# Self-attention: one PSUM bank moves from the rotation of the first scores to that of the second scores

## The chip, the cores and the metric

The kernel runs on one core of a Trainium2 chip. The metric is the device time of one execution in microseconds, given as the median of several executions. TensorE (PE in the profile) multiplies, VectorE (DVE) and ScalarE (ACT) read its results from PSUM, GpSimd (POOL) works on SBUF only, and SyncE (SP) issues most of the DMAs. PSUM has eight banks, each 128 partitions of 512 float32 values; the stage in question uses all eight.

## What is computed

One decoder block over 4 sequences of 512 tokens, 512 channels wide. The change touches the causal self-attention alone: 32 heads of 16 channels, in 8 groups of 4 heads that share keys and values.

```python
x = x + attn(layernorm(x))          # self-attention: the stage with the change
x = x + xattn(layernorm(x), ctx)    # cross-attention, 8 heads
x = x + ffn(layernorm(x))           # quantised feed-forward

# attn, per sequence b and group g:
scores = jnp.einsum('bqgjd,bkgd->bgjqk', q, k) / np.sqrt(HD)
scores = jnp.where(qpos[:, None] < qpos[None, :], -jnp.inf, scores)
w = jax.nn.softmax(scores, axis=-1)
ctx = jnp.einsum('bgjqk,bkgd->bqgjd', w, v).reshape(b, s, D) @ Wo.T
```

## The kernel before

The program is a chain of stages: projection of q, k, v (tiles named `a_`), self-attention (`b_`), output projection (`c_`), cross-attention (`d_`), feed-forward (`e_`). Each is a block of its own, and each engine has its instructions written out by hand in a fixed order. Engines meet only in semaphores.

Self-attention computes each score tile twice. The **first scores** (query rows on the partitions) exist only to find each row's maximum. The **second scores** (keys on the partitions) are computed again, with the negated maxima as two extra rows of the contraction, so that ScalarE can take the exponential and write the weights in the layout in which TensorE needs them.

There are 32 steps of first scores, one for each pair of sequence and group, and a software pipeline five steps deep. In iteration `i` of the loop (called step `i` below) the engines do:

- first scores of step `i`: ten units U0 to U9. TensorE (L609) fills one PSUM bank `b_p1` with a unit (one 512-wide tile, two of 256, or one of 128 and one of 384); VectorE (L584) adds the mask, takes the row maxima, and frees the bank (`p1_used`). U0 and U1 are F(0) and F(1) in the code, and so on.
- TURN, the transposition of the maxima of step `i - 1` (L617), which VectorE reads as two rows `b_mrow` (L576, L578). SyncE copies these into the query tile `b_qs` for the second scores of the next step.
- OUT, the transposition of the outputs of step `i - 4` (L624), which VectorE divides by the row sums (L564, L568). TURN and OUT use banks of the same rotation `b_p1`.
- second scores of step `i - 2`: eleven units S(0) to S(10) in banks `b_p2` (L638, and L641 for the diagonal masks), each read by one exponential on ScalarE (L531), which frees the bank (`exps`).
- weighting of the values with step `i - 3`: sixteen matmuls W(0) to W(3) in the one bank `b_pv` (L653), without a break; ScalarE then copies that bank to `b_osb` (L541).

VectorE takes the banks of the first rotation in this order:

```python
        ORDER = [0, 1, OUT, 2, TURN] + list(range(3, NU))
```

TensorE's order in one step, in which F waits for a free `b_p1` bank and S for a free `b_p2` bank, is:

```python
                F(0); S(0); F(1); S(1)
                turn_outputs()
                F(2); S(2)
                turn_maxima()
                F(3); S(3)
                F(4); S(4)
                W(0); W(1); W(2); W(3)
                F(5); S(5); F(6); S(6); F(7); S(7); F(8); S(8); F(9); S(9); S(10)
```

A unit may be filled when the unit that stands one rotation's length ahead of it in VectorE's order has been read. With four banks F(4) waits for OUT, since the order there is OUT, 2, TURN, 3, 4.

In the traces both rotations are called `b_p`, because numbers of buffers are left out: the line tells them apart (L609, L617 and L624 write the first rotation, L638 and L641 the second). PEld rows are weight loads; the wait of a matmul stands before its weight load.

Of the kernel before, what the change touches and what calls it, by code (L numbers as in the profile page):

```python
# [397 lines left out]
def self_attention(nc, io, scr, keep):  # L398


    STEPS = BATCH * GROUPS
    BANKS1, BANKS2 = 4, 3
    with ExitStack() as ctx:
        m = Store(nc, ctx, "b", keep["semaphores"])
        qs = m.sb("qs", [P, UNROLL, GSZ, SEQ], BF16)
# [951 lines left out]
def decoder(nc, io, out):  # L1357
# [9 lines left out]
    with ExitStack() as ctx:  # L1367
        def sb(name, shape, dt=F32):
            return ctx.enter_context(nc.sbuf_tensor(name, shape, dt))

        def sems(name, n):
            return [ctx.enter_context(nc.semaphore(f"{name}{k}")) for k in range(n)]
        keep = {
            "semaphores": ctx,


            "dve_passed": ctx.enter_context(nc.semaphore("dve_passed")), "pool_passed": ctx.enter_context(nc.semaphore("pool_passed")),
            "ident": sb("ident", [P, P]), "identb": sb("identb", [P, P], BF16), "ones64": sb("ones64", [P, XROWS]),
            "mask_qk": sb("mask_qk", [P, SEQ], BF16), "mask_kq": sb("mask_kq", [P, GSZ, P], BF16),
            "wscale": sb("wscale", [P, 3]), "winv": sb("winv", [P, 3]), "minus_half": sb("minus_half", [P, TPB]), "wo_hi": sb("wo_hi", [P, KD, DIM], F32R), "wo_lo": sb("wo_lo", [P, KD, DIM], F32R),  # L1380

            "v": sb("v", [P, BATCH * GROUPS, TPB, 2 * HDIM]),
        }
        project_qkv(nc, io, scr, keep)

        keep.update(wg=sb("wg", [P, KD, FF], BF16), wu=sb("wu", [P, KD, FF], BF16), wd=sb("wd", [P, KF, DIM], BF16))
        self_attention(nc, io, scr, keep)

        keep.update(k2=sb("k2", [P, 2, DIM]), qh=sb("qh", [P, UNROLL, DIM], F32R), ql=sb("ql", [P, UNROLL, DIM], F32R),
                    k_in=sems("k_in", 2), q_in=sems("q_in", UNROLL))  # L1390
        output_projection(nc, io, scr, keep)

        keep.update(ffn_x=sb("ffn_x", [P, XSLOTS, DIM]), ffn_x_in=sems("ffn_x_in", UNROLL))
        cross_attention(nc, io, scr, keep)
        feed_forward(nc, io, scr, keep, out)
# [32 lines left out]
```

## Time and profile before

| | us |
|---|---|
| median of 3 runs | 911.53 |
| lowest and highest | 908.85, 912.01 |
| the profiled execution | 906.05 |
| its span | 904.2 |
| PE busy | 789.2 (87%) |
| VectorE busy | 696.3 (77%) |
| ScalarE busy | 453.7 (50%) |

The span runs from the first to the last instruction, and 1.85 us of the profiled execution's time lie around it. Busy shares are means over five stages with different limits, so they say little on one stage; self-attention takes the stretch from about 101 to 403 us. Rows of the timeline give the start in us, the duration in us, the engine, the line, what is written and read, and in brackets how long the engine sat idle before it and what ended that.

### The profile page before, as it was taken

The numbers are of one execution on the slowest core, as the hardware profiler recorded it, in microseconds if no ns is written. First come the engines' busy times: TensorE is split into PE (matmuls) and PEld (weight loads), VectorE is DVE, ScalarE is ACT, GpSimd is POOL, SyncE is SP. The second block draws the span as 40 slices with busy tenths as digits, with TensorE's granted clock in tenths as the row PEclk, the third lists the DMA queues.
The fourth block names the chain that finished last, engine by engine and source line by source line (L and its number), as shares of the span: only waits on it lengthen the run. The fifth ranks groups of instructions, "written<-read, shape, count | busy, mean of one in ns | idle before, by whom it ended". The sixth has DMA issues, their size and how long they took to land. (4 is left out here: it accounts for less than half of the span.)

```text
span 904.2 us, 14319 instructions
## 1 busy us (share of the span) xinstructions
PE 789.2 (87%) x4306; PEld 404.1 (45%) x4306; DVE 696.3 (77%) x1982; ACT 453.7 (50%) x791; POOL 410.4 (45%) x412
## 2 busy tenths in 40 slices
PE   2999589999999999977884899999998379999997
PEld 1888334444444444436662444434433034444443
DVE  7554489888888889814775899898986478989984
ACT  2566147666776767652222555445544134455442
POOL 1556399999940000001223576667666323433331
PEclk9999779999999999998996899999999789999999
DMA  7987545555523223116995555655552224445443
GB/s 265 345 285 250 184 130 169 153 168 147 145 58 85 71 72 81 40 32 217 315 326 192 146 152 158 177 154 158 159 165 80 72 51 94 106 113 112 126 99 94
DMA packets 137101, 134.46 MB, mean 149 GB/s; under 512 B 87232, under 2 KB 99136, under 8 KB 133952
## 3 DMA queue, kind: packets, MB, share of 16 engines
q1 hardware_dynamic: 111488, 104.18, 39.6%
q10 hardware_dynamic: 23808, 16.78, 6.6%
q0 software_dynamic: 1728, 12.58, 4.2%
q8 instruction: 35, 0.57, 0.3%
q14 instruction: 42, 0.34, 0.1%
HBM read 89.65 MB, written 33.03 MB: 136 GB/s over the span
## 5 line engine op out<-in xcount | busy, mean ns | idle before, releaser
L584 DVE CUSTOM_DVE_ANT_0 b_junk<-b_p,mask_qk 128x128 bf16<-128x128 f32 (+3 forms) x512 | 217.7, 483 | 34.6 <-PE b_p L609 34.3
L531 ACT ACTIVATE b_probs<-b_p 128x512 f32<-128x512 f32 (+1 forms) x352 | 176.7, 560 | 49.0 <-PE b_p L641 27.2
L609 PE MATMUL b_p<-b_ks,b_qs 96*128 96x128 bf16 (+3 forms) x512 | 127.5, 314 | 16.0 <-DMA b_ks<-k_parts 10.0
L971 ACT ACTIVATE d_probs<-d_p 128x512 f32<-128x512 f32 x128 | 74.3, 594 | 106.5 <-PE d_p L1077 106.5
L638 PE MATMUL b_p<-b_qs,b_ks 98*128 98x512 bf16 (+1 forms) x352 | 123.0, 364 | 2.8 <-DMA b_qs<-b_mrow 1.8
L944 POOL TENSOR_TENSOR d_halves<-d_probs 128x1024 f32<-128x1024 f32 x32 | 76.2, 2382 | 54.0 <-ACT d_probs L971 53.9
L730 POOL TENSOR_SCALAR c_veps<-c_mv 128x1 f32<-128x1 f32 x16 | 7.1, 446 | 204.2 <-DVE c_mv L779 204.2
L995 DVE TENSOR_REDUCE d_mx<-d_p 128x1 f32<-128x512 f32 x128 | 83.7, 670 | 18.6 <-PE d_p L1060 17.5
L1341 PE MATMUL e_pg<-wg,e_xt 128*128 128x512 bf16 x256 | 67.0, 385 | 18.7 <-DMA e_xt<-e_xq 18.7
L609 PEld LDWEIGHTS b_p<-b_ks,b_qs 96*128 96x128 bf16 x512 | 45.3, 100 | 81.5 <-DVE b_mx L584 19.5
L1060 PE MATMUL d_p<-d_kk,qh 128*128 128x512 f32 x128 | 62.3, 493 | 21.6 <-DVE d_kk L1010 12.4
L653 PE MATMUL b_pv<-b_probs,v 128*32 128x512 f32 (+3 forms) x1024 | 75.5, 436 | 0.0
L1222 ACT ACTIVATE e_silu<-e_pg,e_cg 128x512 f32<-128x512 f32 x64 | 42.0, 680 | 63.9 <-PE e_pg L1341 63.9
L1106 PE MATMUL d_pn<-d_probs,d_vt 128*64 128x512 f32 x256 | 69.1, 622 | 0.0
L1341 PE MATMUL e_pu<-wu,e_xt 128*128 128x512 bf16 x256 | 66.6, 383 | 0.0
L1004 DVE RECIPROCAL d_rden<-d_pd 128x128 f32<-128x128 f32 x64 | 59.6, 938 | 7.0 <-PE d_pd L1095 6.6
L1060 PEld LDWEIGHTS d_p<-d_kk,qh 128*128 128x128 f32 x128 | 25.6, 202 | 85.2 <-issue 47.5
L1206 POOL TENSOR_SCALAR e_h<-e_h,e_fh 128x1024 f32<-128x1024 f32 x32 | 38.7, 1221 | 53.6 <-DVE e_fh L1323 53.6
L1353 PE MATMUL e_pd<-wd,e_ht 128*128 128x512 bf16 x256 | 57.7, 379 | 2.4 <-DMA e_ht<-e_hq 2.4
L1256 DVE TENSOR_TENSOR e_h<-e_pu,e_silu 128x512 f32<-128x512 f32 x64 | 43.9, 686 | 14.1 <-ACT e_silu L1222 9.6
L1076 PE MATMUL d_p<-qh,d_kk 128*128 128x512 f32 x128 | 52.4, 409 | 0.0
L1077 PE MATMUL d_p<-ql,d_kh 128*128 128x512 f32 x128 | 51.8, 405 | 0.0
(141 smaller groups left out, 1512.0 us busy)
## 6 DMA issues: line engine op xcount, KB each, us to landing
k<-in_ctx SPq DMA_DIRECT2D x64, 128.0 KB, 2.6
qh<-x_normed_high SPq DMA_DIRECT2D x64, 128.0 KB, 2.8
q_parts<-a_parts SPq DMA_DIRECT2D x16, 384.0 KB, 4.3
b_qs<-q_parts SPq DMA_DIRECT2D x32, 192.0 KB, 3.4
a_x<-in_x SPq DMA_DIRECT2D x4, 1024.0 KB, 5.6
a_wst<-in_w_gate SPq DMA_DIRECT2D x4, 1024.0 KB, 6.8
a_wst<-in_w_up SPq DMA_DIRECT2D x4, 1024.0 KB, 8.5
a_wst<-in_w_down SPq DMA_DIRECT2D x4, 1024.0 KB, 8.5
```

The source lines that it names most:

```text
L531: nc.scalar.activation(pblock(j % 2, kb)[:, j0:j0 + nj, c:c + w], p2[(NE * j + n) % BANKS2][:, 0:nj * w].rearrange("p (j c) -> p j c", j=n ...
L584: best = nc.vector.tensor_tensor_reduce(out=junk[:, 2 * ((NU * i + k) % BANKS1) + n, 0:w], in0=bank[:, c:c + w], in1=keep["mask_qk"][:, SE ...
L609: last = nc.tensor.matmul(p1_bank(i, k)[:, c:c + w], qs[0:STACK, s, j, qt * P:(qt + 1) * P], ks[0:STACK, s, 0:w], start=True, stop=True)
L638: last = nc.tensor.matmul(bank, ks[0:STACK + 2, s, kb * P:(kb + 1) * P], qs[0:STACK + 2, s, j0:j0 + nj, kb * P + c:kb * P + c + w], start= ...
L653: last = nc.tensor.matmul(pv[2 * HDIM * j:2 * HDIM * (j + 1), kb * P:], v, pblock(j3 % 2, kb)[:, j, :], start=kb == 0, stop=kb == TPB - 1, ...
L944: nc.gpsimd.tensor_tensor(halves[:], probs[:, s4, 0:2, :], probs[:, s4, 2:4, :], ALU.add).then_inc(halved, 1)
L971: nc.scalar.activation(probs[:, s3, n, :], p2[(KD * s3 + n) % BANKS][:], ACT.Exp, scale=SCALE).then_inc(exps, 1)
L995: nc.vector.reduce_max(mx[:, s1 % 2, n:n + 1], p1_bank(u, use_of(n))[:], AX.X).then_inc(p1_used, 1)
L1004: nc.vector.reciprocal(rden[:, s, at], pd[:, at]).then_inc(rden_done, 1)
L1060: nc.tensor.matmul(p1_bank(u, k)[:], qh[:, s1, n * P:(n + 1) * P], kk[:, s1, :], start=True, stop=True).then_inc(p1_full, 1)
L1106: last = nc.tensor.matmul(pn[a % 2 * H:(a % 2 + 1) * H, :], vt[:, a, nb, :], probs[:, a, nb, :], start=nb == 0, stop=nb == KD - 1, skip_gr ...
L1341: last = nc.tensor.matmul(bank[g % BANKS][:], xt[:, j % 2, k, :], keep[w][:, k, n * 512:(n + 1) * 512], start=k == 0, stop=k == KD - 1)
```

## The change

The first rotation gets three banks and the second four. The order of instructions on every engine stays as it is. What moves is which earlier reading each filling waits for. The index of VectorE's junk output, which nothing reads, also goes by `BANKS1`.

```diff
@@ -399,7 +399,7 @@
     STEPS = BATCH * GROUPS
-    BANKS1, BANKS2 = 4, 3
+    BANKS1, BANKS2 = 3, 4
```

The uses that follow from it, unchanged in their text (L595 to L597, L635 to L637):

```python
                def bank_free(k):
                    if due(USE[i, k] - BANKS1 + 1):
                        pe.wait_ge(p1_used, USE[i, k] - BANKS1 + 1)
...
                    if due(unit - BANKS2 + 1):
                        pe.wait_ge(exps, unit - BANKS2 + 1)
                    bank = p2[unit % BANKS2][:, 0:nj * w]
```

The instructions with their waits, in the program's order, differ on TensorE alone and only where a rotation is used for the first time. This is the first of the two places, in step 0, the fourth unit of first scores:

```order
 L609 MATMUL b_p<-b_ks,b_qs 128x512
 L609 MATMUL b_p<-b_ks,b_qs 128x256 x2
-L609 MATMUL b_p<-b_ks,b_qs 128x128
+L609 MATMUL b_p<-b_ks,b_qs 128x128 [waits b_p1_used]
 L609 MATMUL b_p<-b_ks,b_qs 128x384
 L609 MATMUL b_p<-b_ks,b_qs 128x512 [waits b_p1_used]
```

There the fourth unit has to wait where it had a fresh bank before. Everywhere else the same waits stand at the same instructions, with the count on the first rotation one unit higher and that on the second one unit lower. For the middle of a step this is, by the code, what each filling waits for:

| filling | before: after VectorE has read | after: after VectorE has read |
|---|---|---|
| OUT | U8 of the step before | U9 of the step before |
| F(2) | U9 of the step before | U0 |
| TURN | U0 | U1 |
| F(3) | U1 | OUT |
| F(4) | OUT | U2 |
| F(5) | U2 | TURN |

## Rows read from the trace of the kernel before

**Rows 1.** Busy time by stretch: start of self-attention, its steady part, its end.
```profile
core 0: us, PE busy (x) PEld busy (x) DVE busy (x) ACT busy (x) POOL busy (x), PEclk, DMA share, GB/s
100.00:134.00 34.00, 23.95 (x115) 9.25 (x116) 26.49 (x119) 8.12 (x17) 22.28 (x26) 0.65 0.57 167
134.00:381.00 247.00, 239.70 (x1905) 114.55 (x1903) 217.18 (x1008) 172.04 (x337) 117.80 (x131) 1.00 0.40 109
381.00:410.00 29.00, 20.65 (x164) 9.07 (x162) 6.57 (x26) 15.45 (x32) 0.00 (x0) 0.90 0.23 58
```

**Rows 2.** Timeline of VectorE through one step, 302.9 to 311.6.
```profile
302.87 0.29 DVE L584 CUSTOM_DVE_ANT_0 b_junk<-b_p,mask_qk 128x128 bf16<-128x128 f32 x1 [0.94 <-PE b_p L609]
...
306.87 0.08 DVE L584 DVE_READ_ACCUMULATOR2_ANT b_mx<- 128x1 f32 x1
...
307.48 0.08 DVE L584 DVE_READ_ACCUMULATOR2_ANT b_mx<- 128x1 f32 x1
...
307.77 0.42 DVE L568 TENSOR_TENSOR b_o<-b_p,b_rec 128x256 f32<-128x256 f32 x1
...
308.11 0.41 DVE L584 CUSTOM_DVE_ANT_0 b_junk<-b_p,mask_qk 128x256 bf16<-128x256 f32 x1
...
308.80 0.08 DVE L584 DVE_READ_ACCUMULATOR2_ANT b_mx<- 128x1 f32 x1
308.80 0.27 DVE L576 TENSOR_SCALAR b_mrow<-b_p 16x128 bf16<-16x128 f32 x1
...
309.31 0.27 DVE L584 CUSTOM_DVE_ANT_0 b_junk<-b_p,mask_qk 128x128 bf16<-128x128 f32 x1
...
310.00 0.67 DVE L584 CUSTOM_DVE_ANT_0 b_junk<-b_p,mask_qk 128x512 bf16<-128x512 f32 x1
...
310.61 0.07 DVE L584 DVE_READ_ACCUMULATOR2_ANT b_mx<- 128x1 f32 x1
...
311.61 0.29 DVE L584 CUSTOM_DVE_ANT_0 b_junk<-b_p,mask_qk 128x128 bf16<-128x128 f32 x1 [0.93 <-PE b_p L609]
```

**Rows 3.** Timeline of TensorE in the same step: F(2), TURN, F(3), F(4), W(0), F(5).
```profile
306.84 0.38 PE L609 MATMUL b_p<-b_ks,b_qs 96*128 96x256 bf16 x2
...
307.22 0.27 PE L617 MATMUL b_p<-ident,b_mx 128*16 128x128 f32 x1
...
307.62 0.11 PEld L609 LDWEIGHTS b_p<-b_ks,b_qs 96*128 96x128 bf16 x2 [0.46 <-DVE b_mx L584]
...
308.25 0.10 PEld L609 LDWEIGHTS b_p<-b_ks,b_qs 96*128 96x128 bf16 x1 [0.46 <-DVE b_o L568]
...
308.74 2.36 PE L653 MATMUL b_pv<-b_probs,v 128*32 128x512 f32 x32
...
311.03 0.39 PE L609 MATMUL b_p<-b_ks,b_qs 96*128 96x128 bf16 x2
```

**Rows 4.** The copies of b_pv on ScalarE, one a step; steps 3, 31, 32 and 34.
```profile
133.76 0.60 ACT L541 ACTIVATE b_osb<-b_pv 128x512 f32<-128x512 f32 x1 [1.83 <-PE b_pv L653]
...
381.00 0.60 ACT L541 ACTIVATE b_osb<-b_pv 128x512 f32<-128x512 f32 x1 [1.83 <-PE b_pv L653]
...
388.45 0.60 ACT L541 ACTIVATE b_osb<-b_pv 128x512 f32<-128x512 f32 x1 [1.60 <-PE b_pv L653]
...
401.17 0.60 ACT L541 ACTIVATE b_osb<-b_pv 128x512 f32<-128x512 f32 x1 [1.99 <-PE b_pv L653]
```

**Rows 5.** A step in which a load came late, at 217.8.
```profile
217.79 0.11 PEld L609 LDWEIGHTS b_p<-b_ks,b_qs 96*128 96x128 bf16 x2 [1.65 <-DMA b_ks<-k_parts]
```

**Rows 6.** Second scores waiting for an exponential: S(10) in a steady step, S(8) near the end.
```profile
304.78 0.10 PEld L638 LDWEIGHTS b_p<-b_qs,b_ks 98*128 98x128 bf16 x1 [0.19 <-ACT b_probs L531]
...
389.62 0.39 PE L638 MATMUL b_p<-b_qs,b_ks 98*128 98x512 bf16 x1 [0.25 <-ACT b_probs L531]
```

**Rows 7.** Groups by line and shape, 134 to 381 (count, busy us, mean ns, idle before).
```profile
L531 ACT ACTIVATE b_probs<-b_p 128x384 f32<-128x384 f32 x112 | 54.8, 489 | 16.5 <-PE b_p L638 12.7
...
L584 DVE CUSTOM_DVE_ANT_0 b_junk<-b_p,mask_qk 128x128 bf16<-128x128 f32 x112 | 31.7, 283 | 27.1 <-PE b_p L609 27.1
```

## Prediction before the run

> **What bounds the kernel now.** The change acts in self-attention only, so I first looked at busy time by stretch [rows 1]. In the steady part, 134 to 381 us, PE is drawn busy for 239.70 of 247.00 us and VectorE for 217.18; ScalarE with 172.04 has room. A busy PE is no proof of a bound, because the profile draws matmuls with their pipeline's length and they overlap. So the question is where each of the two stands idle, and for whom.
>
> The groups by line answer for VectorE: its 128-wide maxima have 27.1 us of idle time before them, all of it ended by a first score [rows 7]. The timeline of one step shows that this is one gap a step and nothing else: 0.94 us before the piece at 302.87, none until 310.68, and 0.93 us before the piece at 311.61 [rows 2]. That piece belongs to U5, the first unit after the weighting. VectorE thus works 7.8 us and stands 0.93 us in a period of 311.61 - 302.87 = 8.74 us.
>
> TensorE in the same step [rows 3] waits twice just ahead of the weighting: F(3) sits 0.46 us until maxima are read, F(4) sits 0.46 us until `b_o` is written, and starts at 308.25. The weighting follows at 308.74 and runs unbroken to F(5) at 311.03, and U5 reaches VectorE at 311.61. In those 2.3 us TensorE fills no bank for VectorE, which drains the four it has and then stands.
>
> So neither engine is the bound alone. The period is a ring: VectorE ends OUT (307.77 + 0.42 = 308.19), F(4) starts 0.06 later, W, F(5), U5 on VectorE, and from there VectorE's own unbroken work until it ends OUT again. Its sum is (311.61 - 308.19) + (308.19 - 302.87) = 3.42 + 5.32 = 8.74 us, the period. Any delay of F(4) lengthens it; a wait elsewhere does so only if it leaves VectorE without a full bank.
>
> **The change part by part.** Nothing is added or removed: no instruction, no DMA, no queue order. Only the waits bind to other units.
>
> *F(4), the term that decides.* It now waits for U2 instead of OUT. U2 is read as two pieces from 308.11, and the reading of its last accumulator ends at 308.80 + 0.08 = 308.88 [rows 2]. With the same 0.06 us of signalling F(4) starts at 308.94 instead of 308.25 [rows 3], 0.69 us later. S(4), the sixteen weighting matmuls and F(5) stand behind it on the same in-order engine, and U5 on VectorE waits for F(5). The ring becomes 3.42 + 5.32 + 0.69 = 9.43 us. VectorE's gap grows from 0.93 to 1.62 us; nothing hides it, as VectorE already stands idle there. The copies of `b_pv` at 133.76 and 381.00 are the first and the last of 29 (two of them shown) that belong to steps in which F(4), W and F(5) all occur, steps 3 to 31 [rows 4]. **29 x 0.69 = +20.0 us.**
>
> *The other fillings of the first rotation.* I replayed them by adding 0.06 us to the end of the new predecessor and comparing the result, plus the 0.58 us from F(5)'s start to U5's start (311.03 to 311.61) [rows 2, 3], with the moment at which VectorE comes to the unit:
> - F(2) waits for U0, whose accumulator is read until 306.95: 307.01 instead of 306.84, full by 307.59; wanted at 308.11.
> - TURN waits for U1 (307.56): 307.62 instead of 307.22, full by 308.0 (0.27 us long, and some 0.1); wanted at 308.80.
> - F(3) waits for OUT (308.19): 308.25 instead of 307.62, full by 308.83; wanted at 309.31.
> - F(4) at 308.94, full by 309.52; wanted at 310.00.
>
> All four have some 0.5 us in hand, and the units before and after them more or about as much. So these waits cost nothing: VectorE's unbroken work from U5 to U4 covers them. Without that cover the tightest would cost its excess, which is the third rival.
>
> *The second rotation.* With four banks S(10) no longer waits 0.19 us for an exponential in a steady step [rows 6], and ScalarE stands less before its 384-wide exponentials (16.5 us in all, [rows 7]). In the steady part I price this at nothing: S(10) stands where VectorE has full banks in hand, so TensorE's being 0.2 us earlier only lengthens its lead. If that cover were absent it would be worth 29 x 0.19 = 5.5 us. **0; bounds -5.5 and 0.**
>
> *The end of the stage.* From step 32 on there are no first scores. The period is 7.45 us there (388.45 - 381.00), and S does wait for exponentials, 0.25 us at 389.62 [rows 4, 6]. One more bank lets S(4), and so the weighting, start up to one exponential earlier; a 384-wide one takes 0.49 us [rows 7]. I take 0.2, 0.4 and 0.5 us for the three last weightings: **-1.1 us; bounds -1.5 and 0.**
>
> *The late loads.* From 133.76 to 381.00 are 28 periods, 247.24 us [rows 4], where 28 x 8.74 = 244.7. The 2.5 us over are a few steps in which a load for TensorE came late; the worst waited 1.65 us at the weight load [rows 5]. SyncE issues these loads when units of the step before are done, and they are wanted a step later, so a period longer by 0.69 us gives each that much more time. Most of them vanish and the worst shrinks: **-2.0 us; bounds -2.5 and 0.**
>
> *The first steps.* Steps 0 to 2 have no weighting. They wait for loads and for the slow TensorE clock (0.65 granted on the mean, [rows 1]), and VectorE there is fed unit by unit. Three banks still hold two while one is refilled. I take **+0.3 us**; bounds 0 and 3 x 0.69 = 2.1, as if each lost one unit's wait.
>
> **Sum**: 20.0 - 1.1 - 2.0 + 0.3 = +17.2 us. The profiled execution took 906.05 us, so a like one should take 923.3. That execution was 5.5 us below the median of the three runs (911.53), a scatter that I can't assign to this stage, so I add the sum to the median: **928.7 us**, 1.9% slower.
>
> **A rule weighed against the trace.** In the steady part the granted clock is 1.00, TensorE's 2.4 GHz, although TensorE has two short waits in each step; in the stretch before it, with PE drawn busy 23.95 of 34.00 us, it is 0.65, a mixture of 2.4 and 1.2 GHz [rows 1]. The Trainium skill (TensorE: Matmul & The Clock Gate, section "A second HAM failure mode: psum-queue depth-cycling") says that a kernel which cycles through PSUM banks can idle so often between groups of matmuls that its clock swings between the two levels. That speaks against this change, which makes those idle times longer. By the row the cost is nothing; by the rule it would be that of the second rival below. The new waits are 0.7 us a step in a step that keeps its 8 us of work, far nearer to the steady row than to the one before it, so I go by the row.
>
> **The rivals.**
> 1. *The freed wait of the second scores was the bound (faster).* For it: TensorE does wait for exponentials each step, and ScalarE stands 12.7 us for 384-wide second scores [rows 6, 7]. It would give -5.5 - 1.1 = -6.6 us, 904.9 us. Against it: VectorE has no idle time between U5 and U4, so a late S(10) can't be on the ring. It decides only if F(4) comes to its place after U2's end anyway, that is if TensorE ran 0.7 us later before W than the trace has it.
> 2. *The clock falls.* If TensorE fell to half speed its step would be bound by its own work: 8.74 less some 0.6 us of true waiting is about 8 us, so 16 us, 7 us more than 9.4. One step in ten (three steps) would bring 21 us: 950 us, and more if more often. For it: the first stretch. Against it: 1.00 throughout 247 us.
> 3. *VectorE runs dry at a second place.* If one of the fillings above comes 0.5 us later than my replay, VectorE loses perhaps 0.3 us more a step: +8.7, 937 us. For it: the spare time is only 0.5 us, less than one 512-wide reduction (0.67 us, [rows 2]). Against it: the order has S units of some 0.2 us between, and before this the same spaces never opened a gap.
> 4. *The new wait doesn't bind.* If something that I haven't seen held F(4) back equally before, or the end of the stage waited for other work, the change would be within 0.5% of before: about 911 us. Against it: the weight load of F(4) names `b_o` as its releaser [rows 3], and GpSimd is idle after 381 us [rows 1].
>
> **How the numbers follow.** What a measurement of this kernel can tell from no change is about 0.5%, 4.6 us. I give the forecast 0.81, rival 1 0.03, rival 2 0.05, rival 3 0.07 and rival 4 0.04. The forecast's own range: all bounds low, but for the -5.5 us, which is rival 1's, give 20.0 - 1.5 - 2.5 = 16.0, all high 20.0 + 2.1 = 22.1, so 927.5 to 933.6; with the scatter of the runs (908.85 to 912.01) 924 to 935. The range of 8 in 10 reaches from there a little to rivals 3 and 4: 921 to 937. Slower by over 0.5%: forecast and rivals 2 and 3, 0.93. Faster: 0.03. Same: 0.04.
>
> **What would show it right or wrong.** In the timeline of the changed kernel the idle time of VectorE before U5 should be 1.6 us, once a step, and the group of 128-wide maxima should show about 29 x 0.69 more idle time, some 47 us. F(4)'s weight load should name `b_mx` instead of `b_o`; F(3)'s should name `b_o`. The copies of `b_pv` should come 9.43 us apart. The wait of S(10) should be gone and the clock remain at 1.00. The prediction fails if those copies are still 8.7 us apart (rival 1 or 4), if a second gap stands in VectorE's step (rival 3), or if the granted clock of the steady part falls below 1.00 (rival 2).

## The result, and the profile after

Seven banks split three and four take 925.97 us (median of 6 runs, 923.43 to 930.51); before takes 908.62 us (median of 6, 907.27 to 912.01, the three runs shown ahead of the prediction among them). The ratio is 1.0187, 95% interval 1.0154 to 1.0221: 17.35 us slower. The profiled execution took 923.43 us with a span of 921.6.

Busy time by stretch of the changed kernel, which answers to [rows 1] (the steady part now ends near 400 us):

```profile
100.00:134.00 34.00, 23.67 (x100) 7.63 (x105) 26.65 (x119) 8.05 (x16) 22.06 (x25) 0.65 0.55 166
134.00:400.00 266.00, 248.43 (x1895) 111.69 (x1916) 216.90 (x1008) 172.69 (x337) 118.38 (x131) 1.00 0.37 101
```

VectorE does the same 217 us of work in 266 us that it did in 247. TensorE's granted clock is 1.00 as before. The two groups by line and shape that answer to [rows 7], with the weight loads of the first scores (count, busy us, mean ns, idle before):

```profile
L531 ACT ACTIVATE b_probs<-b_p 128x384 f32<-128x384 f32 x110 | 53.8, 489 | 35.0 <-PE b_p L638 35.0
...
L609 PEld LDWEIGHTS b_p<-b_ks,b_qs 96*128 96x128 bf16 x445 | 36.5, 97 | 67.6 <-DVE b_mx L584 25.3 <-DVE b_o L568 12.9 <-issue 6.1
...
L584 DVE CUSTOM_DVE_ANT_0 b_junk<-b_p,mask_qk 128x128 bf16<-128x128 f32 x111 | 31.4, 283 | 45.3 <-PE b_p L609 45.3
```

The idle time before the 128-wide maxima rose from 27.1 to 45.3 us. One step of the timeline shows where; it answers to [rows 2, 3]. The weight loads are those of F(2), TURN, F(3) and F(4), then come the weighting and F(5), then U5 on VectorE:

```profile
310.25 0.11 PEld L609 LDWEIGHTS b_p<-b_ks,b_qs 96*128 96x128 bf16 x2 [0.21 <-DVE b_mx L584]
...
310.92 0.09 PEld L617 LDWEIGHTS b_p<-ident,b_mx 128*16 128x16 f32 x1 [0.45 <-DVE b_mx L584]
...
311.49 0.11 PEld L609 LDWEIGHTS b_p<-b_ks,b_qs 96*128 96x128 bf16 x2 [0.48 <-DVE b_o L568]
...
312.04 0.08 DVE L584 DVE_READ_ACCUMULATOR2_ANT b_mx<- 128x1 f32 x1
...
312.17 0.10 PEld L609 LDWEIGHTS b_p<-b_ks,b_qs 96*128 96x128 bf16 x1 [0.51 <-DVE b_mx L584]
...
312.66 2.36 PE L653 MATMUL b_pv<-b_probs,v 128*32 128x512 f32 x32
...
314.95 0.39 PE L609 MATMUL b_p<-b_ks,b_qs 96*128 96x128 bf16 x2
...
315.53 0.29 DVE L584 CUSTOM_DVE_ANT_0 b_junk<-b_p,mask_qk 128x128 bf16<-128x128 f32 x1 [1.62 <-PE b_p L609]
...
318.02 0.38 PE L609 MATMUL b_p<-b_ks,b_qs 96*128 96x128 bf16 x2
```

F(4) sits until U2's last accumulator is read (312.04 + 0.08), starts 0.05 later, and U5 finds VectorE idle for 1.62 us instead of 0.93. The releasers moved as the table of the change says: F(3) names `b_o`, F(4) names `b_mx`.

The copies of `b_pv`, which answer to [rows 4]: two neighbours of the steady part, the last of it (step 31), and steps 32 to 34:

```profile
305.67 0.60 ACT L541 ACTIVATE b_osb<-b_pv 128x512 f32<-128x512 f32 x1 [1.83 <-PE b_pv L653]
315.09 0.60 ACT L541 ACTIVATE b_osb<-b_pv 128x512 f32<-128x512 f32 x1 [1.83 <-PE b_pv L653]
...
399.81 0.60 ACT L541 ACTIVATE b_osb<-b_pv 128x512 f32<-128x512 f32 x1 [1.83 <-PE b_pv L653]
...
406.90 0.60 ACT L541 ACTIVATE b_osb<-b_pv 128x512 f32<-128x512 f32 x1 [1.24 <-PE b_pv L653]
...
413.70 0.60 ACT L541 ACTIVATE b_osb<-b_pv 128x512 f32<-128x512 f32 x1 [1.22 <-PE b_pv L653]
...
418.75 0.60 ACT L541 ACTIVATE b_osb<-b_pv 128x512 f32<-128x512 f32 x1 [1.50 <-PE b_pv L653]
```

They give a full account. The first copy (step 3) is at 134.68, before at 133.76. In the table "late" is what the 28 periods from step 3 to 31 take over 28 times the steady period.

| | before | changed | difference |
|---|---|---|---|
| copy of step 3 | 133.76 | 134.68 | +0.92 |
| 28 steady periods | 28 x 8.73 | 28 x 9.41 | +19.0 |
| late | 2.80 | 1.65 | -1.15 |
| step 31 to 34 | 20.17 | 18.94 | -1.23 |
| copy of step 34 | 401.17 | 418.75 | +17.58 |

The spans differ by 17.4 us, so what follows self-attention takes what it took (503.0 us from the copy of step 34 to the end of the span before, 502.9 after). The large terms repeat from trace to trace. The first row and "late" don't: with four and three banks and another order (`turn_first_43`, below) the copy of step 3 is at 134.63, with three and three (`three_three`) at 135.37, and the latter's 28 periods have about 1 us over 28 x 9.41, not 1.65.

### The profile page after: what moved, and what is told of

Its sections match the earlier page's. It is cut to its first block and busy times, and to the rows that moved or that the text cites. A ratio compares the mean times of both kernels' runs of the same rounds, so it can differ in the third digit from the quotient of the medians.

```text
span 921.6 us, 14271 instructions
## 1 busy us (share of the span) xinstructions
PE 793.7 (86%) x4258; PEld 399.5 (43%) x4306; DVE 695.1 (75%) x1982; ACT 454.6 (49%) x791; POOL 411.7 (45%) x412
## 5 line engine op out<-in xcount | busy, mean ns | idle before, releaser
L1341 PE MATMUL e_pg<-wg,e_xt 128*128 128x512 bf16 x250 | 65.9, 384 | 20.0 <-DMA e_xt<-e_xq 19.7
L609 PEld LDWEIGHTS b_p<-b_ks,b_qs 96*128 96x128 bf16 x512 | 42.4, 99 | 92.4 <-DVE b_mx L584 36.7
```

The source lines that it names most:

```text
L609: last = nc.tensor.matmul(p1_bank(i, k)[:, c:c + w], qs[0:STACK, s, j, qt * P:(qt + 1) * P], ks[0:STACK, s, 0:w], start=True, stop=True)
L1341: last = nc.tensor.matmul(bank[g % BANKS][:], xt[:, j % 2, k, :], keep[w][:, k, n * 512:(n + 1) * 512], start=k == 0, stop=k == KD - 1)
```

## The experiments

**Undo half of it.** `three_three` leaves the eighth bank unused.

```diff
-    BANKS1, BANKS2 = 4, 3
+    BANKS1, BANKS2 = 3, 3
```

> Three banks for the first scores, three for the second, the eighth bank unused: half of the change. My theory (the changed kernel's time comes from F(4) waiting for U2, a ring through the weighting): the steady period is that of the changed kernel, 9.41 us between copies of b_pv, and only the gain at the stage's end is lost, so about 1.2 us above the changed kernel, 18 to 20 us above the kernel before. Rival (the fourth bank of the second scores also buys something in the steady part, up to 0.19 us a step): a period up to 9.6 us, 5 to 7 us above the changed kernel.

925.61 us, before 909.13 on the same chip, ratio 1.0192 (1.0163 to 1.0222). The steady period is 9.42 us and the last three steps take 20.18 us (420.11 - 399.93). So the fourth bank of the second scores buys 1.24 us at the end of the stage and nothing in the steady part; the whole loss is the bank taken from the first scores. The medians of this run and the changed kernel, on different chips, are too near to show the 1.2 us (925.61, 925.97); the two traces do.

**Change which unit F(4) waits for, banks untouched.** `turn_first_34` and `turn_first_43` take TURN ahead of unit 2.

```diff
-        ORDER = [0, 1, OUT, 2, TURN] + list(range(3, NU))
+        ORDER = [0, 1, OUT, TURN] + list(range(2, NU))
...
                 turn_outputs()
-                F(2); S(2)
                 turn_maxima()
+                F(2); S(2)
                 F(3); S(3)
```

> The changed kernel (three and four) with TURN moved ahead of unit 2, on TensorE and VectorE alike. The last three fillings before the weighting are then U2, U3, U4 instead of TURN, U3, U4, and F(4) waits for TURN (0.51 us) instead of U2 (0.69 us). My theory: the ring is 0.18 us shorter, a period of 9.23 us, about 5 us below the changed kernel. Rival (what costs is one bank less, not the unit that F(4) waits for): period 9.41, no difference.

> The same move of TURN in the kernel before (four and three). F(4) waits for OUT in both orders, and the four units that VectorE has left for the weighting are the same four. My theory: period 8.73 as before, no difference within 1 us. Rival (TURN's earlier place helps or harms by itself, as through the earlier copy of the maxima): a difference from the kernel before of the same size as that of the run with three and four banks from the changed kernel.

With three and four banks: 919.18 us, ratio to before 1.0110 (1.0080 to 1.0141), where the changed kernel has 1.0187, so 7 us less where 5 were expected. The period accounts for 28 x 0.18 = 5.0 us of it; the rest lies in the first copy and the late loads (step 34's copy is at 412.41 against 418.75) and is within the scatter of such runs. Its copies of `b_pv` and the weight load of F(4) in the timeline:

```profile
301.16 0.60 ACT L541 ACTIVATE b_osb<-b_pv 128x512 f32<-128x512 f32 x1 [1.83 <-PE b_pv L653]
...
307.48 0.10 PEld L609 LDWEIGHTS b_p<-b_ks,b_qs 96*128 96x128 bf16 x1 [0.33 <-DVE b_mrow L578]
...
310.39 0.60 ACT L541 ACTIVATE b_osb<-b_pv 128x512 f32<-128x512 f32 x1 [1.83 <-PE b_pv L653]
...
310.84 0.29 DVE L584 CUSTOM_DVE_ANT_0 b_junk<-b_p,mask_qk 128x128 bf16<-128x128 f32 x1 [1.43 <-PE b_p L609]
```

The period is 9.23 us, as worked out, F(4) names `b_mrow`, and the gap before U5 shrinks by the 0.19 us. With four and three banks the same move leaves the period at 8.73: 907.27 us, ratio 0.9983 (0.9968 to 0.9999). That is 1.9 us below 909.13 where less than 1 was expected; the trace shows no gain in self-attention (copy of step 34 at 402.06, before at 401.17). So with the count of banks unchanged, the period follows the unit that F(4) waits for.

**Take one bank more from the first scores.** `two_four`: two and four, one unused.

> Two banks for the first scores, four for the second, one unused: the suspected cost taken one bank further. My theory: F(4) then waits for TURN, 0.51 us of VectorE's work after U2, so the ring alone gives 9.41 + 0.51 = 9.92 us a step, 15 us above the changed kernel. That is a floor: with two banks a refill (0.06 + 0.58 us) has only one unit of 0.61 to 0.69 us to hide behind and second scores stand between, so VectorE should also run dry at other units, 30 us above the changed kernel or more. Rival (each bank taken away costs about the same, whatever waits): again about 17 us, and VectorE's idle time stays in one gap before U5.

965.09 us, ratio 1.0615 (1.0589 to 1.0642), 39 us over the changed kernel's 925.97. The steady period is 10.63 us, 0.71 above the floor of 9.92. VectorE's named idle times of one step, and its last reading of TURN:

```profile
301.94 0.29 DVE L584 CUSTOM_DVE_ANT_0 b_junk<-b_p,mask_qk 128x128 bf16<-128x128 f32 x1 [1.88 <-PE b_p L609]
...
305.65 0.29 DVE L584 CUSTOM_DVE_ANT_0 b_junk<-b_p,mask_qk 128x128 bf16<-128x128 f32 x1 [0.17 <-PE b_p L609]
...
307.24 0.26 DVE L564 RECIPROCAL b_rec<-b_p 128x16 f32<-128x16 f32 x1 [0.20 <-PE b_p L624]
...
308.87 0.28 DVE L578 SCALAR_TENSOR_TENSOR b_mrow<-b_p,b_mrow 16x128 bf16<-16x128 f32 x1
```

With three banks there was one gap; with two there are more. From U5 to the end of TURN VectorE takes 7.21 us (301.94 to 309.15), and in the kernel before 6.51 (302.87 to 309.38, the reading of TURN starting at 309.10). These 0.70 us are pauses elsewhere than before U5, two of them long enough to be named above, and F(4), which waits for TURN, is released that much later: they are the 0.71 above the floor. This is the rival "VectorE runs dry at a second place", at two banks and not at three.

**Take banks from the second scores.** `four_two` (one unused) and `five_two`, the change's opposite, which also gets ten junk slots instead of eight, so that no two maxima share one.

> Four banks for the first scores, two for the second, one unused: takes a bank from the other rotation. S(10) then waits for the exponential of S(8) instead of S(7), 0.52 us later on ScalarE, and F(0) stands behind it. TensorE's lead over VectorE there is some 0.3 us, so VectorE stands 0.2 to 0.4 us a step at U0: a period of 9.0 to 9.1, 8 to 11 us above the kernel before, plus 1 to 2 us at the stage's end. Rival (a bank of the second rotation buys nothing in the steady part at any count, as from three to four): period 8.73.

> Five banks for the first scores, two for the second: the change's opposite. F(4) waits for U1 instead of OUT, 0.63 us earlier, so the ring through the weighting alone would give 8.73 - 0.63 = 8.1 us, and VectorE's own work is 7.8. But S(10) waits for a later exponential, as in the run with four and two banks. My theory: the late second scores are then the bound, a period of 8.8 to 9.1, between 2 and 10 us above the kernel before. Rival (only the first rotation matters): 8.1 to 8.3 us, 12 us or more below the kernel before.

`four_two`: 922.11 us, before 908.63, ratio 1.0157 (1.0131 to 1.0183). `five_two`: 919.45 us, ratio 1.0126 (1.0090 to 1.0163). Steady periods 9.18 and 8.92 us; steps 31 to 34 take 23.53 us in both, 3.4 more than before. The timeline of `four_two`:

```profile
302.31 0.10 PEld L638 LDWEIGHTS b_p<-b_qs,b_ks 98*128 98x128 bf16 x1 [0.61 <-ACT b_probs L531]
...
303.33 0.29 DVE L584 CUSTOM_DVE_ANT_0 b_junk<-b_p,mask_qk 128x128 bf16<-128x128 f32 x1 [0.36 <-PE b_p L609]
...
308.77 0.29 DVE L584 CUSTOM_DVE_ANT_0 b_junk<-b_p,mask_qk 128x128 bf16<-128x128 f32 x1 [0.93 <-PE b_p L609]
```

The gap before U5 is that of before; a second one of 0.36 us opens at U0, behind a second score that waited 0.61 us for an exponential. In `five_two` the gap before U5 falls to 0.67 us, but the same 0.35 us stands at U0. I had the sign and the place right, the period by 0.1 us too low in `four_two`, and the cost at the stage's end at half its size in `four_two` and not at all in `five_two`, which is 10.8 us above before where 2 to 10 were expected. The second rotation is flat from three to four and steep from three to two.

**Break the block that F(4) stands in front of.** `split_34` and `split_43`:

```diff
                 turn_outputs()
+                W(0)
                 F(2); S(2)
                 turn_maxima()
                 F(3); S(3)
+                W(1)
                 F(4); S(4)
-                W(0); W(1); W(2); W(3)
+                W(2); W(3)
```

> The changed kernel (three and four), but TensorE's weighting is no longer one block of 2.3 us: W(0) stands behind OUT, W(1) behind S(3), W(2) and W(3) behind S(4). The same matmuls, the same waits. My theory (VectorE stands only because no bank is filled in one long block): no piece is over 0.9 us, VectorE's gap of 1.62 us mostly closes, and the step is bound by TensorE's own work, some 8.1 to 8.4 us; 29 to 38 us below the changed kernel, 11 to 20 us below the kernel before. Rival (three banks cost by themselves, through waits at each filling): a period above 9 us and slower than the kernel before.

> The kernel before (four and three) with the same split weighting. My theory: the same bound by TensorE's own work, 8.1 to 8.4 us a step; 10 to 18 us below the kernel before, and within 2 us of the run with three and four banks (which has the stage's end in its favour by 1.2 us). The cost of the change, 17 us, should be gone once the weighting is split. Rival (bank cost by itself): three and four banks still about 17 us slower than this one.

`split_34` 909.95 us, ratio to before 1.0021 (0.9986 to 1.0057); `split_43` 911.14 us, 1.0024 (0.9993 to 1.0055). Periods 8.71 and 8.68 us. The bank's cost went from 0.68 us a step to 0.03: this half of my theory holds. The gain over before didn't come: `split_34` is 16 us below the changed kernel, not 29 to 38. TensorE's timeline in `split_34` shows why; these rows are W(0), F(2), then S(2), TURN and S(3), then W(1), F(4), W(2) with W(3), F(5):

```profile
307.46 1.07 PE L653 MATMUL b_pv<-b_probs,v 128*32 128x512 f32 x8
...
308.46 0.39 PE L609 MATMUL b_p<-b_ks,b_qs 96*128 96x256 bf16 x2
...
308.69 0.33 PE L638 MATMUL b_p<-b_qs,b_ks 98*128 98x384 bf16 x1
...
308.86 0.27 PE L617 MATMUL b_p<-ident,b_mx 128*16 128x128 f32 x1
...
309.19 0.33 PE L638 MATMUL b_p<-b_qs,b_ks 98*128 98x384 bf16 x1
...
309.44 0.85 PE L653 MATMUL b_pv<-b_probs,v 128*32 128x384 f32 x8
...
310.23 0.39 PE L609 MATMUL b_p<-b_ks,b_qs 96*128 96x512 bf16 x1
...
310.71 0.86 PE L653 MATMUL b_pv<-b_probs,v 128*32 128x256 f32 x16
...
311.50 0.39 PE L609 MATMUL b_p<-b_ks,b_qs 96*128 96x128 bf16 x2
```

From start to start the pieces take 1.00 + 0.79 + 0.79 = 2.58 us, the block 2.29 [rows 3]. Each break adds about 0.15 us there. It also costs ahead of a piece: S(3) takes 0.25 us from its start to that of W(1), where S(2), of the same shape, takes 0.17 to TURN's. TensorE's matmuls follow each other without a pause in this step, so its own work is now the bound. I had left the breaks out of that work (8.1 to 8.4 expected, about 8.7 found). VectorE still stands, 0.47 us before U5 and 0.36 us at U2, but behind a busy TensorE. In `split_43` late loads add to it; more on them below.

**One break less.** `two_pieces_43` puts W(0) behind TURN and keeps W(1) to W(3) behind S(4); `two_pieces_34` has three and four banks and W(0) behind OUT.

> Four and three banks, the weighting in two pieces: W(0) behind TURN, W(1) to W(3) behind S(4). In three pieces TensorE had no idle time left in a step of 8.68 us, and the pieces took 2.58 us instead of 2.29: each break costs some 0.15 us. Two pieces should save one break: a period of 8.5, 4 to 7 us below the kernel before if the late loads don't grow. Rival (the break isn't what costs): 8.7.

> Three and four banks, the weighting in two pieces: W(0) behind OUT, W(1) to W(3) behind S(4). F(4) still waits for U2 and 1.3 us of weighting still stand behind it. The ring of the changed kernel less W(0)'s 0.9 us would be 8.5, but W(0) now stands ahead of F(2) and F(2) to F(4) come later: I expect 8.6 to 8.9, 14 to 22 us below the changed kernel and about as the kernel before, and 3 to 10 us above the run with four and three banks in two pieces: with a larger block the bank still costs. Rival (any break closes the gap as in three pieces): within 2 us of it.

`two_pieces_43`: **902.27 us**, before 908.13, ratio 0.9944 (0.9914 to 0.9974), the fastest version with the full computation. Its step:

```profile
298.21 0.60 ACT L541 ACTIVATE b_osb<-b_pv 128x512 f32<-128x512 f32 x1 [0.97 <-PE b_pv L653]
...
298.66 0.29 DVE L584 CUSTOM_DVE_ANT_0 b_junk<-b_p,mask_qk 128x128 bf16<-128x128 f32 x1 [0.64 <-PE b_p L609]
...
306.65 0.60 ACT L541 ACTIVATE b_osb<-b_pv 128x512 f32<-128x512 f32 x1 [0.97 <-PE b_pv L653]
```

The period is 8.44 us, the gap before U5 0.64. TensorE is busy throughout, as it is with three pieces; busy time by step, first `two_pieces_43`, then `split_43`:

```profile
298.21:306.65 8.44, 8.44 (x70) 4.08 (x69) 7.74 (x36) 6.05 (x13) 0.00 (x0) 1.00 0.33 78
...
301.03:309.71 8.68, 8.68 (x70) 3.94 (x69) 7.82 (x36) 6.16 (x12) 0.00 (x0) 1.00 0.30 73
```

So the second break costs 8.68 - 8.44 = 0.24 us a step, not the 0.15 that I had read from the pieces alone, and TensorE's own work with the unbroken block would be about 8.44 - 0.24 = 8.20 us (an estimate), which is inside my 8.1 to 8.4. The 28 periods gain 28 x 0.29 = 8.1 us; the late loads take 3.0 back (5.85 us over 28 regular periods, 2.80 before).

`two_pieces_34`: 917.69 us, ratio 1.0098 (1.0063 to 1.0133), period 9.01, above my 8.6 to 8.9. I placed it rightly between the changed kernel and the other, but it is only 8 us below the changed kernel (14 to 22 expected) and 15 above `two_pieces_43` (3 to 10 expected): W(0) ahead of F(2) did more harm than I allowed:

```profile
307.87 0.42 DVE L584 CUSTOM_DVE_ANT_0 b_junk<-b_p,mask_qk 128x256 bf16<-128x256 f32 x1 [0.35 <-PE b_p L609]
...
308.70 0.10 PEld L609 LDWEIGHTS b_p<-b_ks,b_qs 96*128 96x128 bf16 x1 [0.75 <-DVE b_mx L584]
```

VectorE stands 0.35 us at U2, and F(4), which waits for U2, inherits that. The two differ in where W(0) stands as well as in banks, so their 0.57 us a step is not the price of the bank alone.

**What makes loads late.** `two_loads_43` and `two_loads_split_43` drop ten of GpSimd's twelve 1 MB loads from the kernel before and from `split_43`. Both leave out most of the feed-forward's weights, so they serve as measurements only.

```diff
-                    if c + 1 < 3 * LOADS:
+                    if c + 1 < 2:
                         load(c + 1)
-                    pool.wait_ge(wst_in[c % 2], 16 * (c // 2 + 1))
+                    pool.wait_ge(wst_in[c % 2], 16)
```

> The kernel before, without ten of the twelve 1 MB loads of feed-forward weights that GpSimd issues during self-attention (the feed-forward then works with two slices of weights only; the number of instructions on the compute engines is unchanged). In both traces all late loads of the attention's own tiles lie between 106 and 243 us, where these 1 MB loads are issued, one each 12.4 us. My theory: they are what makes the others late; without them the 28 periods from step 3 have next to no excess over 28 x 8.73 (2.8 us before) and the first steps gain 1 to 2 us: 3 to 5 us below the kernel before. Rival (late by their own queue's order on SyncE): the excess stays at 2 to 3 us.

> The same omission in the run with four and three banks and the weighting in three pieces, whose 28 periods had 9.9 us of excess over 28 x 8.68. My theory: the excess goes, the steady period stays 8.68, and the time falls by 8 to 12 us. Rival (late by their own queue's order): excess stays near 10 us.

904.95 us, ratio 0.9961 (0.9943 to 0.9979), and 902.72 us, ratio 0.9939 (0.9919 to 0.9959), both to before. The excess of `split_43` was 9.9 us in its profile and is 0.0 here, with the period at 8.68. GpSimd's own work is not what changed: from 134 to 170 us it is busy for 33.95 us in the kernel before and for 34.02 without the loads.

Not all of the 9.9 us is waiting. Two steps hold 7.7 of it, 12.71 and 12.37 us long, and in both the granted clock fell. This is the busy time of the first, and the weighting W(0) in it:

```profile
152.27:164.98 12.71, 10.65 (x70) 4.14 (x69) 8.09 (x36) 6.16 (x13) 12.00 (x14) 0.87 0.50 157
...
159.18 1.94 PE L653 MATMUL b_pv<-b_probs,v 128*32 128x512 f32 x8
```

TensorE had stood 1.95 us for a load just before 157.32. Then the granted clock fell to 0.50 (1.2 GHz) between 160 and 162 us, and W(0) took 1.94 us instead of 1.06. TensorE was busy for 10.65 us in this step, where the regular one has 8.68; in the second (granted clock 0.86) for 10.47, after a stand of 1.90 us. So some 3.8 of the 9.9 us are the slower clock, which a sum of the waits misses. Without the 1 MB loads the granted clock is 1.00 from 134 us on. In `two_pieces_43` a stand of 2.13 us left the clock at 1.00, so such a stand doesn't always lower it.

In the kernel before the excess falls from 2.8 to 0.93 us. The 0.93 left sits in the same four steps in six of the nine runs with the weighting in one block (not in `two_four`, `four_two` and `five_two`). In the one of these steps that I looked at, in the kernel before, 0.22 of its 0.31 us is a pause inside VectorE's stretch that no engine or load ends:

```profile
242.35 0.69 DVE L584 CUSTOM_DVE_ANT_0 b_junk<-b_p,mask_qk 128x512 bf16<-128x512 f32 x1 [0.22 <-issue]
```

So of "late" in the table above, some 1.9 us before and, if the same 0.93 stays, 0.7 us after were loads that those 1 MB loads delay. What the pause is stays open.

## Why the prediction was right

- **F(4) and the ring.** Predicted 29 x 0.69 = 20.0 us and a period of 9.43; measured 9.41 against 8.73, so 28 x 0.68, and the 29th is in the copy of step 3: 19.7 us. The experiments back the cause and not only the size: three and three banks give the same period, moving TURN changes it by just the difference of the two units' durations with three banks and not at all with four, and cutting the weighting up removes the cost.
- **The other fillings cost nothing.** Replayed starts, with the changed times shifted by 3.25 us (U5, which opens the step, was at 302.87 before and is at 315.53 - 9.41 = 306.12 here): F(2) 307.00 for 307.01, TURN 307.67 for 307.62, F(3) 308.24 for 308.25, F(4) 308.92 for 308.94. VectorE has one gap a step. The spare 0.5 us was real, and one bank further it was gone.
- **The second rotation in the steady part: 0.** Right. S(10)'s wait of 0.19 us [rows 6] is gone, and yet F(0) starts 3.07 us after F(5) (318.02 - 314.95), as in the kernel before (305.36 - 302.29):

```profile
302.29 0.39 PE L609 MATMUL b_p<-b_ks,b_qs 96*128 96x128 bf16 x2
...
305.36 0.38 PE L609 MATMUL b_p<-b_ks,b_qs 96*128 96x128 bf16 x2
```

That wait stood on a weight load and delayed nothing that the step rests on. With `three_three`, whose period is the same with one bank less there, this refutes the first rival.
- **The stage's end: -1.1 us.** Measured -1.23.
- **The late loads: -2.0 us.** Measured -1.15 between these two traces. I took the whole 2.5 us over the regular step (2.80, against 8.73) for late loads. But 0.93 us of it sits in four steps that a longer period doesn't mend, so 1.9 us at most could come back. Of these 1.2 did here and about 1.7 in `three_three` at the same period; the size of this term isn't known better than that.
- **The first steps: +0.3 us.** The copy of step 3 is 0.92 later; less F(4)'s 0.69 that is 0.23. That it fits is luck: this copy moves by 0.7 to 0.9 us between runs with the same period (134.63 in `turn_first_43`, 135.37 in `three_three`).
- **The clock** stayed at 1.00 with the added waits, so the rule of the Trainium skill on cycling through PSUM banks (TensorE: Matmul & The Clock Gate, section "A second HAM failure mode: psum-queue depth-cycling") found no case here; in the run with two banks, whose waits are longer still, it is 1.00 as well. It did fall in `split_43`, but after single stands of 1.9 us for a load, not with the short waits for banks.

The errors nearly cancel: the ring 0.3 too high, the late loads' return 0.85 too high, the stage's end 0.1 too low; 17.2 predicted, 17.4 between the spans and 17.35 between the medians. The mechanism earns an agreement to about 1 us; the closeness beyond that is luck, since the interval of the ratio is 14 to 20 us. The predicted 928.7 us lies 2.7 above the median mostly because three more runs moved the median of before from 911.53 to 908.62.

## What to carry to other kernels

In this kernel the number of banks that a rotation needs is set by the longest stretch in which the producer fills none: the consumer must have that much work in full banks when it begins. Find the filling that stands in front of that stretch, and price a bank by the duration of the one unit by which its wait moves. That price holds as long as the other fillings keep spare time: from four to three banks it gave 0.69 us for a measured 0.68, from three to two 0.51 for 1.21. If the block can be cut, cut it as few times as the banks demand, since each cut costs TensorE time too, here 0.24 us. One cut gained 0.6%; two gained nothing, in part because late loads took more, for without the 1 MB loads the version with two cuts is 2 us faster than the one with none (902.72 and 904.95).

## What I had not expected

- Breaking the run of 16 float32 matmuls among bf16 ones costs TensorE about 0.24 us a break: 0.15 in the pieces (2.58 against 2.29 us for three), the rest ahead of a piece. What in the change of matmuls costs this stays open.
- 1 MB weight loads on GpSimd's queue, one each 12.4 us, delay the small loads of SyncE's queue enough to hold a weight load of TensorE by over 2 us, and two such stands were followed by a slower clock: 9.9 us of excess in the profile of `split_43`, none without them. A faster step seems to make it worse, but that is not shown: the excess was 1.65 us at a period of 9.41, 2.8 at 8.73, 3.9 and 9.9 at 8.71 and 8.68, 5.85 at 8.44, and 4.6 at 9.01, one execution each. This is the longest such wait in the steady part of `split_43` (`two_pieces_43` has one of 2.62 us):

```profile
157.32 0.11 PEld L609 LDWEIGHTS b_p<-b_ks,b_qs 96*128 96x128 bf16 x2 [2.45 <-DMA b_ks<-k_parts]
```
